# The end of a two-layer perceiver kernel split by batch, with one eviction rule and one order of queries changed

## The chip, the cores and the metric

One core of a Trainium2 chip runs the whole program. The metric is the device time of one execution in microseconds, as the median of several. TensorE (PE), VectorE (DVE), ScalarE (ACT), GpSimd (POOL) and SyncE (SP, which only starts transfers here) run side by side and wait for each other by semaphores; there is no other order between them.

## The reference, cut to what matters

Two layers over x of 2 batches x 128 rows x 256 columns. All edits lie in layer 1 (and the last part of layer 0's feed-forward stands just ahead of it).

```python
x = x + _L1_xattn_ref(_layernorm(x), ctx_2048, ...)   # 16 heads of 16, all 4096 context keys, int8-like rounding
x = x + _L1_attn_ref(_layernorm(x), ...)              # two positions per row, causal: row 0 sees itself only
x = x + _L1_ffn_ref(_layernorm(x), ...)               # router, shared MLP of 1024, routed MLP of 128
return x
# _L1_attn_ref: position 0 of the causal pair has output = its own value; position 1 needs q, both k, both v
# _L1_ffn_ref:
logits = x @ router_weight.T
topk_vals, topk_idx = top_k(logits, 2)
comb_w = sum(softmax(topk_vals) * (topk_idx < 8))
shared = (g * sigmoid(g) * u) @ sh_down.T             # g, u = x @ sh_gate.T, x @ sh_up.T
routed = (same with r_gate, r_up, r_down) * comb_w
```

In the self-attention of layer 1 the two batches of the kernel are the two positions. So batch 0 needs only its own value, while batch 1 needs its queries and the keys and values of both.

## The kernel before, in words

The kernel is written out by hand: each engine has one list of instructions, in the order in which its function bodies (L600 to L2071) issue them. An engine never overtakes itself; a wait at the head of a list stops all that stands behind it.

**Ahead of the attention (L1841 to L1883).** `columns(k, b)` turns the normalised rows `xn` of batch b by two transposes and ScalarE copies them (L728) to `xnT`. `queries(b)` (L1846) multiplies them with the query weights; `integer_queries(b)` on VectorE (L1357) rounds them; `query_columns(b)` turns them. `value_rows(n)` (L1854) turns eight blocks of the values, and ScalarE copies them out (L973). The TensorE order is columns(3,0), value_rows(0), queries(0), value_rows(1), columns(3,1), value_rows(2), query_columns(0), queries(1), then scores(0,0). ScalarE copies columns(3,0), then runs one dummy exponential at L968, which loads the table for what follows, then goes on to L973.

**The cross-attention (L1885 to L1978).** A unit is one head of one batch, `UNITS` = 32 of them, batch the faster index. Per unit: `scores(u, c)` for four chunks of 1024 keys (two products of 512 columns each, L1897), read on VectorE by `maxima(u, c)` (L1387), which scales, keeps the maximum and stores; GpSimd combines the four maxima (L693 to L697); ScalarE makes the exponentials as bytes (L1002); a quarter (c = 0, 1, 2) is turned by TensorE in `turned_over` (L1921) and the last quarter by a DMA transpose started by SP (L583). The turned quarters stand in PSUM in three banks used in turn and are moved out by `columns16`, either on VectorE (L1398) or on ScalarE (L1017); `on_vector(u, c)` (L77) says which. `weighted(u, c)` (L1929 to L1948) multiplies them with the values: 8 products when VectorE moved the quarter (it subtracts 1024 on the way) and 16 when ScalarE did (the subtraction is then done by 8 products with -1024). VectorE works on maxima two units ahead of the quarter that TensorE turns. SP also brings the scales of head h+2 (L568, two halves of 1 MB) as the buffer of head h becomes free.

**Behind the attention (L1981 to L2071 on TensorE, L1415 to L1486 on VectorE, L1027 to L1060 on ScalarE).** Everything starts once unit 31 is done. The reciprocals of all 32 sums, both batches' rows scaled (L1420), turned (L1985), copied (L1029), multiplied by the output weights (L1991), added to `xres` (L1429), normalised (add, stats at L1079, aggregate, GpSimd's power at L609, scale at L1071), turned (L1499), copied (L728), then the five products of the self-attention (L1997). Batch 1's attention is VectorE work (L1435 to L1453) with one exponential (L1047). Then each batch goes through turn (L2017), copy (L1043), output product (L2024), add (L1458), normalise, turn, copy, logits (L2044). Only then come the experts: nine steps k (routed block first, then eight shared blocks), each with gate and up products over 256 columns, which are both batches (L2058, 8 records), a tanh on ScalarE (L1060), two VectorE instructions (L1475, L1477). They use four PSUM banks in turn. The routed down product is L2063, the shared one L2069 for batch 0 and then batch 1; VectorE adds them to `xres` and SP writes it out.

`awake(n)` (L1490) issues n products of 512 columns whose result nobody reads. There are 29 of them behind the attention, in six places.

## Time and profile before

| | us |
|---|---|
| runs shown | 439.37 to 440.07, median 439.52 |
| the profiled execution, whole | 442.38 |
| its span | 440.6 |
| PE busy | 408.4 (93%) |
| DVE busy | 357.3 (81%) |
| ACT busy | 303.0 (69%) |
| POOL busy | 105.3 (24%) |

The whole execution is 1.78 us longer than the span, which runs from the first to the last instruction. Busy time of PE counts the full depth of each product, and products overlap, so its 93% does not say that it is at its limit. Times in rows are microseconds from the start of the span; "x16" is how many instructions a row merges; what stands in square brackets is the idle time of the engine before the row and what ended it.

### The profile page before, as it was taken

The numbers are of one execution on the slowest core, as the hardware profiler recorded it, in microseconds if no ns is written. First come the engines' busy times: TensorE is split into PE (matmuls) and PEld (weight loads), VectorE is DVE, ScalarE is ACT, GpSimd is POOL, SyncE is SP. The second block draws the span as 40 slices with busy tenths as digits, with TensorE's granted clock in tenths as the row PEclk, the third lists the DMA queues.
The fourth block names the chain that finished last, engine by engine and source line by source line (L and its number), as shares of the span: only waits on it lengthen the run. The fifth ranks groups of instructions, "written<-read, shape, count | busy, mean of one in ns | idle before, by whom it ended". The sixth has DMA issues, their size and how long they took to land.

```text
span 440.6 us, 9345 instructions
## 1 busy us (share of the span) xinstructions
PE 408.4 (93%) x3822; PEld 297.9 (68%) x3822; DVE 357.3 (81%) x582; ACT 303.0 (69%) x382; POOL 105.3 (24%) x177
## 2 busy tenths in 40 slices
PE   8989899999999999999789999999999999888897
PEld 4878778855555554576347777777777777755686
DVE  2846662879999999987899999999999999654343
ACT  3245834788888776553789999999999999811110
POOL 3100402044444444001245333321111111100000
PEclk9999999999999999999989999999999999889899
DMA  7898912411001100369488789999999894300000
GB/s 281 295 425 301 196 70 73 192 32 31 25 27 27 31 3 0 140 227 438 210 243 249 251 274 263 243 255 251 250 220 311 203 273 101 51 1 0 1 1 24
DMA packets 48245, 71.46 MB, mean 162 GB/s; under 512 B 38954, under 2 KB 41674, under 8 KB 42698
## 3 DMA queue, kind: packets, MB, share of 16 engines
q1 hardware_dynamic: 47626, 67.32, 51.4%
q0 software_dynamic: 576, 3.54, 2.1%
q8 instruction: 30, 0.49, 0.5%
q14 instruction: 13, 0.11, 0.1%
HBM read 61.58 MB, written 1.15 MB: 142 GB/s over the span
## 4 chain that ended last, share of the span: by engine, by line
PE 43%; DVE 41%; issue 7%; ACT 4%; DMA 3%; SPq 1%; DVEq 0%; ACTq 0%
DVE arena L1387 20%; DVE w L1387 9%; PE ps L1671 6%; PE ps L1781 5%; PE ps L1680 5%; PE ps L2058 4%; DVE arena L1398 3%; PE ps L1564 2%; PE ps L1628 2%; DMA arena<-in_segg 2%; PE ps L1720 2%; PE ps L2069 2%; PE ps L1588 1%; PE ps L1493 1%; PE ps L1837 1%
## 5 line engine op out<-in xcount | busy, mean ns | idle before, releaser
L1387 DVE CUSTOM_DVE_ANT_0 arena<-ps,arena 128x1024 f32<-128x1024 f32 x88 | 107.5, 1277 | 0.1
L1897 PE MATMUL ps<-arena 128*128 128x512 bf16 x256 | 77.6, 384 | 11.0 <-DVE arena L1387 7.4
L1002 ACT ACTIVATE arena<-arena 128x4096 uint8<-128x4096 f32 x21 | 78.0, 3716 | 7.8 <-POOL arena L697 7.8
L1921 PEld LDWEIGHTS ps<-cst,arena 128*128 128x128 f32 x384 | 48.2, 144 | 23.2 <-ACT arena L1002 7.2
L1921 PE MATMUL ps<-cst,arena 128*128 128x128 f32 x384 | 59.8, 280 | 2.7 <-ACT arena L1017 2.1
L1941 PE MATMUL ps<-vrow,arena 128*128 128x16 f16 x806 | 52.6, 170 | 0.5 <-ACT w L1017 0.5
L1941 PEld LDWEIGHTS ps<-vrow,arena 128*128 128x128 f16 x806 | 49.2, 96 | 3.9 <-ACT w L1017 0.6
L1387 DVE CUSTOM_DVE_ANT_0 w<-ps,arena 128x1024 f32<-128x1024 f32 x40 | 49.6, 1276 | 0.0
L1944 PE MATMUL ps<-vrow,arena 128*128 128x16 f16 x768 | 45.8, 170 | 0.0
L672 POOL TENSOR_TENSOR arena<-arena 128x1024 f32<-128x1024 f32 x14 | 33.0, 2358 | 39.2 <-DVE arena L1276 39.2
L1944 PEld LDWEIGHTS ps<-vrow,arena 128*128 128x128 f16 x768 | 40.9, 98 | 1.4 <-DVE arena L1398 0.3
L1002 ACT ACTIVATE arena<-w,arena 128x4096 uint8<-128x4096 f32 x10 | 37.1, 3714 | 3.6 <-POOL arena L697 3.6
L693 POOL TENSOR_SCALAR arena<-arena 128x1 f32<-128x1 f32 x32 | 11.7, 366 | 113.8 <-DVE arena L1387 113.7
L1276 DVE TENSOR_TENSOR_SCAN arena<-arena 128x1024 f32<-128x1024 f32 x16 | 37.2, 2363 | 0.2
L1017 ACT ACTIVATE arena<-ps 128x512 f32<-128x512 f32 x70 | 36.9, 589 | 0.0
L1671 PE MATMUL ps<-w,arena 128*128 128x256 f32 x128 | 29.4, 380 | 0.2 <-ACT ps L858 0.2
L1680 PE MATMUL ps<-arena,w 128*128 128x512 f32 x64 | 29.4, 600 | 0.0
L1897 PEld LDWEIGHTS ps<-arena 128*128 128x128 bf16 x256 | 15.6, 97 | 19.7 <-DVE arena L1387 9.7
L926 ACT ACTIVATE arena<-arena 128x254 f32<-128x254 f32 x64 | 27.0, 494 | 0.8 <-DVE arena L1257 0.7
L1781 PE MATMUL ps<-arena,cst 128*128 128x512 f32 x60 | 27.2, 594 | 0.3 <-DVE arena L1287 0.3
L1671 PEld LDWEIGHTS ps<-w,arena 128*128 128x128 f32 x128 | 23.9, 190 | 4.2 <-issue 0.5
L609 POOL TENSOR_TENSOR ln_rs<-ln_ve,neghalf 128x1 f32<-128x1 f32 x12 | 6.6, 554 | 74.7 <-DVE ln_ve L1083 74.7
(278 smaller groups left out, 743.8 us busy)
## 6 DMA issues: line engine op xcount, KB each, us to landing
arena<-ks_scr SPq DMA_DIRECT2D x32, 1024.0 KB, 5.6
arena<-in_w SPq DMA_DIRECT2D x1, 4488.0 KB, 22.1
arena<-in_columns SPq DMA_DIRECT2D x4, 1024.0 KB, 7.8
arena<-in_w0b SPq DMA_DIRECT2D x1, 2560.0 KB, 16.7
w<-in_w SPq DMA_DIRECT2D x1, 2286.0 KB, 10.8
arena<-in_w SPq DMA_DIRECT2D x1, 2048.0 KB, 7.7
arena<-in_fill SPq DMA_DIRECT2D x1, 2048.0 KB, 9.1
arena<-bc_scr SPq DMA_DIRECT2D x14, 128.0 KB, 3.0
```

The costliest lines, as they stand in the source:

```text
L672: pool.tensor_tensor(dbx[:, s], u[:, :, :], bcb[:, n % 4, :].unsqueeze(1).broadcast_to([P, ET, T]), ALU.mult)\
L1002: act.activation(out8[:, :, 0], s_sb[u % 3], ACT.Exp, bias=nb[:, u % 3:u % 3 + 1], accum_out=zall[:, u:u + 1]).then_inc(p_ready, 1)
L1017: act.activation(columns.bitcast(F32), bank(4 + n % 3, 0, 512), ACT.Copy).then_inc(ptr_sb[1], 1)
L1276: dve.tensor_tensor_scan(hst[:, s, :], dA[:, s].rearrange("p t n -> p (t n)"), dbx[:, s].rearrange("p t n -> p (t n)"), 0.0, ALU.mult, ALU ...
L1387: dve.tensor_tensor_reduce(s_sb[slot][:, keys], ps[:, 2 * (c % 2):2 * (c % 2) + 2, :].rearrange("p a n -> p (a n)"), ksb[h % 2][:, keys], ...
L1671: mm = pe.matmul(bank(k_at + a, t * D, D), vT[:, c, i * CK + k:i * CK + k + P], w_kv[:, c, 0:D], start=False, stop=(c == CH - 1), skip_gro ...
L1680: mm = pe.matmul(bank(m, 0, CK), w_kv[:, c, D + m * P:D + (m + 1) * P], vT[:, c, i * CK:(i + 1) * CK], start=(c == 0), stop=(c == CH - 1))
L1781: mm = pe.matmul(bank(6 + n, 0, 512), ident, rows[:, n * 512:(n + 1) * 512], start=False, stop=True, skip_group_check=True)
L1897: mm = pe.matmul(bank(2 * (c % 2) + m, 0, 512), qz[h // 8][:, h % 8, b * L:(b + 1) * L], kT[:, h // 8, k:k + 512], start=True, stop=True)
L1921: mm = pe.transpose(bank(4 + n % 3, k * P, P), words[:, w:w + P], ident)
L1941: pe.matmul(bank(7, u * HW, HW), neg1024[:, :], vrow[:, h // 2, v:v + HW], start=False, stop=False)
L1944: mm = pe.matmul(bank(7, u * HW, HW), turned, vrow[:, h // 2, v:v + HW], start=(t == 0), stop=(t == KT - 1))
```

## The change

Three things are changed.

1. `on_vector(u, 0)` is true for even u instead of for u mod 3 < 2 (and stays true for units 30 and 31). For units 0 to 29 that is 15 quarters on VectorE instead of 20; the five others go to ScalarE, with 8 more small products each on TensorE.
2. Ahead of the attention, TensorE issues queries(1), query_columns(0), value_rows(2) instead of value_rows(2), query_columns(0), queries(1). The dummy exponential stands ahead of columns(3,0) on ScalarE.
3. All that follows the attention is written per batch. Batch 0's rows are scaled when unit 30 is done; its turning and its output product stand between the pieces of unit 31, whose result goes to a bank of its own. The self-attention of batch 0 is ahead of batch 1's queries. The experts run as ten steps, five per batch (the routed block alone, then four pairs of blocks, 128 columns each), over two PSUM banks; steps 0 to 4 stand among the instructions of batch 1's self-attention, output and norm. The six `awake` calls (29 products) are replaced by one of three.

```diff
+STEPS = ((FT,), *((m, m + 1) for m in range(0, FT, 2)))
+NS = len(STEPS)
...
-    return (u % 3 < 2 or u >= LAST - 1) if c == 0 else ((u == LAST - 1 and c < TURNED) or (u == LAST and c < 3))
+    return (u % 2 == 0 or u >= LAST - 1) if c == 0 else ((u == LAST - 1 and c < TURNED) or (u == LAST and c < 3))
...
+            act.activation(spare[:, :], spare[:, :], ACT.Exp)
             columns(3, 0)
-            act.activation(spare[:, :], spare[:, :], ACT.Exp)
...
-                for c in range(4 if unit == LAST else TURNED):
+                for c in range(TURNED):
                     if not on_vector(unit, c):
...
+            context_columns(0)
+            columns16(LAST, 3)
+            context_columns(1)
             columns(4, 0)
-            columns(4, 1)
             act.wait_ge(pe_step, VALUE0_MADE)
             act.activation(orow[:, 0, :], bank(5, 0, D), ACT.Copy).then_inc(oa_first, 1)
...
+            def gate_of(k):
+
+                width = len(STEPS[k % NS]) * L
                 act.wait_ge(moe_gu, k + 1)
                 if k >= 2:
                     act.wait_ge(moe_h, k - 1)
-                act.activation(tg[:, k % 2, :], bank(k % 4, 0, T), ACT.Tanh, scale=0.5).then_inc(moe_t, 1)
+                act.activation(tg[:, k % 2, 0:width], bank(k % 2, 0, width), ACT.Tanh, scale=0.5).then_inc(moe_t, 1)
+
+            def shares(b):
+
+                act.wait_ge(te_arg, b + 1)
+                act.activation(te[:, b, :], te[:, b, :], ACT.Exp).then_inc(te_ready, 1)
+
+            self_columns(0)
+            columns(4, 1)
+            act.wait_ge(pe_step, Q_MADE)
+            act.activation(q1[:, :], bank(2, 0, D), ACT.Copy, scale=HW ** -0.5).then_inc(q1_sb, 1)
+            columns(5, 0)
+            act.wait_ge(e2_arg, 1)
+            act.activation(e2[:, :, :], s2[:, :, :], ACT.Exp).then_inc(e2_ready, 1)
+            gate_of(0)
+            shares(0)
+            gate_of(1)
+            self_columns(1)
+            gate_of(2)
+            gate_of(3)
+            columns(5, 1)
+            gate_of(4)
+            shares(1)
+            for k in range(NS, 2 * NS):
+                gate_of(k)
...
+            for unit in range(LAST):
                 for c in range(4):
...
-            columns16(LAST, 1)
-            columns16(LAST, 2)
+            heads = onrm.rearrange("q b (h d) -> q b h d", d=HW)
+            made = bank(7, 0, 512).rearrange("q (h b d) -> q b h d", h=H, b=B)
+            sums, shares = (t.rearrange("q (h b) -> q b h", b=B) for t in (zall, rz))
+
+            def context(b):
+
+                dve.wait_ge(ptr_used, 4 * (LAST + b))
+                link(dve.reciprocal(shares[:, b], sums[:, b]))
+                if b:
+                    dve.tensor_tensor(heads[:, b, H - 1:H], bank(2, 0, HW).unsqueeze(1),
+                                      shares[:, b, H - 1:H].unsqueeze(2).broadcast_to([P, 1, HW]), ALU.mult)
+                n = H - b
+                dve.tensor_tensor(heads[:, b, 0:n], made[:, b, 0:n], shares[:, b, 0:n].unsqueeze(2).broadcast_to([P, n, HW]), ALU.mult)\
+                   .then_inc(on_rows, 1)
+
+            def measured(k, b):
+
+                link(dve.bn_stats(ln_st[:, b, :], xres[:, b, :]))
+                link(dve.bn_aggr(ln_mv[:, b, :], ln_st[:, b, :]))
+                dve.tensor_scalar(ln_ve[:, b:b + 1], ln_mv[:, b, 1:2], EPS, None, ALU.add).then_inc(ln_var, 1)
+
+            def normal(k, b):
+
+                dve.wait_ge(ln_rstd, B * k + b + 1)
+                dve.tensor_scalar(xn[:, b, :], xres[:, b, :], ln_mv[:, b, 0:1], ln_rs[:, b:b + 1], ALU.subtract, ALU.mult)\
+                   .then_inc(ln_rows, 1)
+
+            def crossed(b):
+
+                dve.wait_ge(added_out, (X_OUT0, X_OUT1)[b])
+                link(dve.tensor_tensor(xres[:, b, :], bank((1, 6)[b], 0, D), xres[:, b, :], ALU.add))
+                measured(4, b)
+
+            def attended_self(b):
+
+                dve.wait_ge(added_out, (SA_OUT0, SA_OUT1)[b])
+                link(dve.tensor_tensor(xres[:, b, :], bank((4, 3)[b], 0, D), xres[:, b, :], ALU.add))
+                measured(5, b)
+
+            def routes(b):
+
+                dve.wait_ge(pe_step, (LOGITS0, LOGITS1)[b])
+                link(dve.max(top[:, b, :], bank(7, b * E, E)))
+                dve.tensor_tensor(te[:, b, :], top[:, b, 0:2], top[:, b, 0:1].broadcast_to([P, 2]), ALU.subtract).then_inc(te_arg, 1)
+
+            def weights_of(b):
+
+                dve.wait_ge(te_ready, b + 1)
+                link(dve.tensor_tensor(tz[:, b:b + 1], te[:, b, 0:1], te[:, b, 1:2], ALU.add))
+                link(dve.reciprocal(tz[:, b:b + 1], tz[:, b:b + 1]))
+                link(dve.tensor_tensor(te[:, b, :], te[:, b, :], tz[:, b:b + 1].broadcast_to([P, 2]), ALU.mult))
+                link(dve.tensor_tensor(comb[:, b:b + 1], te[:, b, 0:1], te[:, b, 1:2], ALU.add))
+
+            def hidden(k):
+
+                b, blocks = k // NS, STEPS[k % NS]
+                n = len(blocks)
+                dve.wait_ge(moe_t, k + 1)
+                link(dve.scalar_tensor_tensor(out=ga[:, k % 2, 0:n * L], in0=tg[:, k % 2, 0:n * L], scalar=1.0,
+                                              in1=bank(k % 2, 0, n * L), op0=ALU.add, op1=ALU.mult))
+                dve.scalar_tensor_tensor(out=hT[:, blocks[0]:blocks[0] + n, b * L:(b + 1) * L],
+                                         in0=ga[:, k % 2, 0:n * L].rearrange("p (m l) -> p m l", m=n), scalar=0.5,
+                                         in1=bank(k % 2, T, n * L).rearrange("p (m l) -> p m l", m=n),
+                                         op0=ALU.mult, op1=ALU.mult).then_inc(moe_h, 1)
+
+            def routed(b):
+
+                dve.wait_ge(routed_out, b + 1)
+                link(dve.scalar_tensor_tensor(out=xres[:, b, :], in0=bank((5, 4)[b], 0, D), scalar=comb[:, b:b + 1], in1=xres[:, b, :],
+                                              op0=ALU.mult, op1=ALU.add))
+
+            def finished(b):
+
+                dve.wait_ge(moe_out, b + 1)
+                dve.tensor_tensor(xres[:, b, :], bank((2, 3)[b], 0, D), xres[:, b, :], ALU.add).then_inc(y_ready, 1)
+
+            context(0)
+            for c in range(3):
+                columns16(LAST, c)
             dve.wait_ge(p_ready, UNITS + 2)
...
-            normalise(4, crossed)
+            crossed(0)
+            context(1)
+            normal(4, 0)
+            crossed(1)
+            normal(4, 1)
+            attended_self(0)
+            normal(5, 0)
...
+            routes(0)
...
-            normalise(5, attended_self)
...
+            hidden(0)
+            hidden(1)
+            weights_of(0)
+            hidden(2)
+            attended_self(1)
+            normal(5, 1)
+            hidden(3)
+            hidden(4)
+            routes(1)
+            hidden(NS)
+            weights_of(1)
+            for k in range(NS + 1, 2 * NS):
+                hidden(k)
+            routed(0)
+            finished(0)
+            routed(1)
+            finished(1)
...
+            queries(1)
+            query_columns(0)
             value_rows(2)
-            query_columns(0)
-            queries(1)
...
+                if u == LAST and c == 0:
+                    pe.wait_ge(s_read, 4 * UNITS)
...
+                        out = bank(7, u * HW, HW) if u < LAST else bank(2, 0, HW)
...
+            def context_columns(b):
+
+                pe.wait_ge(on_rows, b + 1)
+                for c in range(CH):
+                    mm = pe.transpose(bank((0, 4)[b], c * P, P), onrm[:, b, c * P:(c + 1) * P], ident)
+                mm.then_inc(pe_step, 1)
+
+            def context_out(b):
+
+                pe.wait_ge(on_cols, b + 1)
+                for c in range(CH):
+                    mm = pe.matmul(bank((1, 6)[b], 0, D), onT[:, c, b * L:(b + 1) * L], w_p[:, c, :],
+                                   start=(c == 0), stop=(c == CH - 1))
+                mm.then_inc(added_out, 1)
+
+            def logits(b):
+
+                pe.wait_ge(ln_cols, 5 * B + b + 1)
+                for c in range(CH):
+                    mm = pe.matmul(bank(7, b * E, E), xnT[:, c, b * L:(b + 1) * L], w_rt[:, c, :],
+                                   start=(c == 0), stop=(c == CH - 1))
+                mm.then_inc(pe_step, 1)
+
+            def gates(k):
+
+                b, blocks = k // NS, STEPS[k % NS]
+                if k >= 2:
+                    pe.wait_ge(moe_h, k - 1)
+                for n, w in ((0, w_sg), (1, w_su)):
+                    for i, m in enumerate(blocks):
+                        for c in range(CH):
+                            mm = pe.matmul(bank(k % 2, n * T + i * L, L), w[:, c, m * P:(m + 1) * P], xnT[:, c, b * L:(b + 1) * L],
+                                           start=(c == 0), stop=(c == CH - 1))
+                mm.then_inc(moe_gu, 1)
+
+            def expert(b):
+
+                pe.wait_ge(moe_h, NS * b + 1)
+                pe.matmul(bank((5, 4)[b], 0, D), hT[:, FT, b * L:(b + 1) * L], w_sd[:, FT, :], start=True, stop=True)\
+                  .then_inc(routed_out, 1)
+
+            def down(b):
+
+                for m in range(FT):
+                    if m % 2 == 0:
+                        pe.wait_ge(moe_h, NS * b + 2 + m // 2)
+                    mm = pe.matmul(bank((2, 3)[b], 0, D), hT[:, m, b * L:(b + 1) * L], w_sd[:, m, :],
+                                   start=(m == 0), stop=(m == FT - 1))
+                mm.then_inc(moe_out, 1)
+
             for c in range(4):
                 weighted(LAST - 1, c)
             turned_over(LAST, 0)
-            for c in range(1, 4):
-                turned_over(LAST, c)
-                weighted(LAST, c - 1)
+            context_columns(0)
+            turned_over(LAST, 1)
+            weighted(LAST, 0)
+            turned_over(LAST, 2)
+            weighted(LAST, 1)
+            pe.wait_ge(wp_scaled, CH)
+            context_out(0)
+            turned_over(LAST, 3)
+            weighted(LAST, 2)
             weighted(LAST, 3)
...
-            awake(5)
...
-            awake(6)
...
-            awake(2)
...
-            awake(8)
...
+            awake(3)
+            context_columns(1)
             columns(4, 0)
...
+            context_out(1)
...
+            projected(0, 2, 5).then_inc(pe_step, 1)
+            projected(0, 1, 3)
+            pe.wait_ge(oa_first, 1)
+            self_columns(0)
             columns(4, 1)
-            projected(0, 2, 5).then_inc(pe_step, 1)
+            self_out(0)
...
             projected(1, 0, 2).then_inc(pe_step, 1)
+            columns(5, 0)
+            logits(0)
+            gates(0)
+            gates(1)
             pe.wait_ge(oa_rows, 1)
             self_columns(1)
+            gates(2)
             self_out(1)
-            awake(5)
-            columns(5, 0)
-            awake(3)
+            gates(3)
+            columns(5, 1)
+            gates(4)
+            logits(1)
+            gates(5)
...
+            expert(0)
+            gates(6)
+            gates(7)
+            expert(1)
+            gates(8)
+            gates(9)
+            down(0)
+            down(1)
```

## Rows read from the trace of the kernel before

**Rows 1.** The chain that ended last, shares of the span by engine.
```profile
PE 43%; DVE 41%; issue 7%; ACT 4%; DMA 3%; SPq 1%; DVEq 0%; ACTq 0%
```

**Rows 2.** Stretch, length, busy (x) of PE PEld DVE ACT POOL, PEclk, DMA, GB/s.
```profile
240.00:260.00 20.00, 18.93 (x303) 14.64 (x302) 20.00 (x34) 19.04 (x17) 6.46 (x15) 1.00 0.84 259
```

**Rows 3.** Groups by line and form, 200 to 380 us: count, busy, mean ns, idle.
```profile
L1387 DVE CUSTOM_DVE_ANT_0 arena<-ps,arena 128x1024 f32<-128x1024 f32 x88 | 107.5, 1277 | 0.1
...
L1387 DVE CUSTOM_DVE_ANT_0 w<-ps,arena 128x1024 f32<-128x1024 f32 x40 | 49.6, 1276 | 0.0
...
L1398 DVE TENSOR_SCALAR arena<-ps 128x1024 f16<-128x1024 f16 x20 | 13.7, 683 | 0.0
```

**Rows 4.** Timeline of one unit: start, duration, engine, line, idle before.
```profile
269.54 1.55 ACT L1017 ACTIVATE arena<-ps 128x512 f32<-128x512 f32 x3
...
270.96 3.72 ACT L1002 ACTIVATE arena<-arena 128x4096 uint8<-128x4096 f32 x1
...
271.76 0.69 DVE L1398 TENSOR_SCALAR arena<-ps 128x1024 f16<-128x1024 f16 x1
...
272.36 1.27 DVE L1387 CUSTOM_DVE_ANT_0 w<-ps,arena 128x1024 f32<-128x1024 f32 x1
...
276.06 3.71 ACT L1002 ACTIVATE arena<-w,arena 128x4096 uint8<-128x4096 f32 x1 [0.32 <-POOL arena L697]
```

**Rows 5.** Timeline ahead of the attention, 206 to 213 us.
```profile
206.03 1.28 ACT L968 ACT_TABLE_LOAD   x1
...
207.43 1.00 ACT L973 ACTIVATE vrow<-ps 128x1024 f16<-128x1024 bf16 x1
...
208.34 0.38 ACT L728 ACTIVATE xnT<-ps 128x256 f32<-128x256 f32 x1
...
209.45 1.08 PE L1850 MATMUL ps<-arena,xnT 128*128 128x256 f32 x4
...
210.57 0.42 DVE L1362 TENSOR_REDUCE arena<-ps 128x16 f32<-128x256 f32 x1 [1.30 <-PE ps L1850]
...
212.64 1.28 DVE L1387 CUSTOM_DVE_ANT_0 arena<-ps,arena 128x1024 f32<-128x1024 f32 x1
```

**Rows 6.** Timeline behind the attention, from unit 31 to the experts.
```profile
384.47 1.95 PE L1921 MATMUL ps<-cst,arena 128*128 128x128 f32 x8
...
389.43 0.18 PE L1941 MATMUL ps<-vrow,arena 128*128 128x16 f16 x1 [0.49 <-ACT w L1017]
...
400.73 0.42 DVE L1435 TENSOR_TENSOR arena<-ps,arena 128x256 f32<-128x256 f32 x1 [3.66 <-PE ps L1997]
...
404.57 0.42 DVE L1453 TENSOR_TENSOR arena<-arena 128x256 f32<-128x256 f32 x1
...
407.95 0.42 DVE L1458 TENSOR_TENSOR xres<-ps,xres 128x256 f32<-128x256 f32 x1 [1.76 <-PE ps L2024]
...
412.69 10.56 PE L2058 MATMUL ps<-xnT,arena 128*128 128x256 f32 x40
```

**Rows 7.** Timeline of the end: experts' steps, down products, last add.
```profile
418.11 0.38 ACT L1060 ACTIVATE arena<-ps 128x256 f32<-128x256 f32 x1 [1.34 <-PE ps L2058]
418.52 0.42 DVE L1475 SCALAR_TENSOR_TENSOR arena<-arena,ps 128x256 f32<-128x256 f32 x1 [0.78 <-ACT arena L1060]
...
430.86 7.07 PE L2069 MATMUL ps<-arena 128*128 128x256 f32 x32
...
437.97 0.42 DVE L1486 TENSOR_TENSOR xres<-ps,xres 128x256 f32<-128x256 f32 x1 [2.96 <-PE ps L2069]
```

**Rows 8.** Timeline: a run of products of 128 columns, 32.7 to 37.2 us.
```profile
32.75 4.37 PE L1564 MATMUL ps<-vrow,arena 128*128 128x128 f32 x36
```

**Rows 9.** Stretches around the two falls of the clock, columns as in Rows 2.
```profile
382.00:388.50 6.50, 6.50 (x112) 5.95 (x110) 3.47 (x6) 3.02 (x6) 0.00 (x0) 0.50 0.00 0
...
389.00:412.50 23.50, 18.95 (x104) 12.11 (x104) 10.75 (x34) 4.27 (x12) 2.21 (x4) 1.00 0.00 1
412.50:416.20 3.70, 3.70 (x12) 3.04 (x13) 1.06 (x7) 0.21 (x1) 0.00 (x0) 0.54 0.00 0
```

140 lines of the change are left out of this document (32 added, 108 removed).

## Prediction

> **What bounds the kernel now.** I read the chain of waits first: PE 43% and DVE 41% of it, so two engines take turns and the question is where [rows 1]. The stretches answer it. From 212.64 us, where the first maximum starts [rows 5], VectorE has no idle time: 20.00 of 20 us while PE, ACT and the DMAs have some left [rows 2]. 128 maxima and 20 turned quarters fill its list, with 0.1 us idle in all [rows 3]. One quarter costs it 0.60 us, from the start of the quarter to the start of the next maximum; the mean of 683 ns in the groups is longer because ends overlap with the next start [rows 3, 4]. Behind the attention the chain is serial: hand-overs between PE, VectorE, ScalarE and GpSimd for batch 1, up to 412.69, then TensorE alone with the experts until 437.97 [rows 6, 7]. So what is worth anything there is work of batch 0 that can be done while batch 1's hand-overs run.
>
> I work out all times on the clock of the profiled execution (span 440.6, whole 442.38) and take the difference off the median of 439.52, which is 2.86 lower than that execution.
>
> **Quarters moved to ScalarE.** 20 - 15 = 5 quarters x 0.60 = 3.0 us off VectorE's list, if nothing else is late. Is ScalarE? Three quarters take it 270.96 - 269.54 = 1.42 us, 0.47 each, and one exponential 3.72 [rows 4]. A unit with two quarters is 4.66 us, with three 5.14; the mean of alternating units is 4.90. VectorE needs 4 x 1.205 = 4.82 or, with a quarter, 5.42, mean 5.12. So ScalarE is 0.3 us late behind each three-quarter unit (5.14 against the 4.82 that VectorE takes then) and gets 0.76 back in the next. Today it does the same every third unit and VectorE does not notice: the exponential at 270.96 comes straight behind three quarters, without a wait, and the next one already waits 0.32 for GpSimd again [rows 4]. TensorE gets 8 products of 16 columns more per moved quarter. Their price is between 0 and that of passes of 128 columns, 0.117 each [rows 8], so at most 0.9 us; I take a quarter of that, since the work of 16 columns is an eighth and something is fixed. It falls into units in which VectorE takes 5.42 us, and in every third unit TensorE does just this today. The DMAs carry the same bytes in a unit 0.1 us shorter: their share of 0.84 [rows 2] goes to 0.86. The bounds: 0 (something just hidden becomes the bound) to 3.0; I take 3.0, since each of the two kinds of unit already stands in today's trace without idle time of VectorE.
>
> **Queries moved up.** VectorE's second rounding starts at 210.57 and waited 1.30 us for TensorE; the product starts at 209.45, so 1.12 lie between [rows 5]. Its operand was copied at 208.34 + 0.38 = 208.72; behind that stood value_rows(2) and query_columns(0), whose inputs came later. Now queries(1) starts right behind the copy: 208.78. And the copy comes earlier: ScalarE ran the table load of 1.28 us at 206.03, in front of the first value rows at 207.43 [rows 5]; with the dummy exponential moved it falls in the idle time before 205.6. The copy at 208.34 then waits only for its transposes, and I put it at 207.96. So queries(1) at 208.4 and the rounding at 209.55: 1.0 us earlier. What is late next is the first rounding, which ends at 209.3, so no more can be had. VectorE goes straight on to the maxima: all of 1.0 us is passed on. Without the earlier copy it is 0.6; bounds 0.6 to 1.1.
>
> Together VectorE ends the maxima 4.0 us earlier. Below I leave these 4.0 out and subtract them at the end.
>
> **Unit 31 with batch 0 in between.** The stretch 382.0 to 388.5 runs at a granted clock of 0.50, that is 1.2 GHz [rows 9]; there eight transposes need 1.95 us, 0.21 each [rows 6]. Batch 0's scaling starts when unit 30's products end (384.6) and takes VectorE 0.7; TensorE waits for it 0.1 and does two transposes, 0.4. The output product is 4 passes, 0.43 each at the low level and 0.215 at the high one (the 32 passes in 7.07 us [rows 7]); with the clock's rise at 388.6 in the middle of them 1.2. The last quarter's product, at 389.43 now [rows 6], starts at 390.5: **1.1 us lost**.
>
> **From there to batch 1's first attention product.** Today 400.73 - 389.43 = 11.3 us [rows 6]. In it both batches' norms alternate on VectorE, and of the five self-attention products three stand between batch 1's turned rows and the keys that VectorE awaits. In the new order batch 0's add and statistics are done in the wait for unit 31, the two products of batch 0 that matter are issued earlier, and in their place batch 0's output product (0.86) stands. I follow it hand-over by hand-over with today's durations (add 0.42, statistics to root 1.4, copy 0.38, four passes 0.86): rows scaled 392.0, output product of batch 1 ready 394.2, its norm 396.2, queries 398.9, keys 399.7, VectorE free at **400.4**. So 0.3 us ahead of today, with the loss already paid. Bounds 399.5 to 401.5.
>
> **Batch 1's attention to its norm.** VectorE's list is the same 3.84 us plus 0.4 for batch 0's router, part of it in the wait for the exponential: rows made at 404.75 + 0.4 (today 404.57 + 0.42 [rows 6], call both 405.0). TensorE in this time does batch 0's logits, step 0 (0.94) and step 1 (1.87). Then gates(2) stands in front of self_out(1): 1.9 us of TensorE that batch 1's chain has to wait out, while the hand-over that it fills takes 0.7. And hidden(2) stands in front of the add on VectorE. The add comes at 408.9 instead of 407.95: **1.0 us lost**. Then the norm, with hidden(3) behind it; TensorE ends gates(3) at 410.1, idles 1.2 us, turns batch 1's rows at 411.3 and begins gates(4) at 411.6.
>
> **What the experts' overlap is worth.** At 411.6 steps 0 to 3 are behind, 0.94 + 3 x 1.87 = 6.55 us of TensorE. What is left: steps 4, 6, 7, 8, 9 at 1.87 = 9.35, step 5 0.94, logits 0.5, two routed products 0.86, down 32 x 0.2155 = 6.9: 18.55 us, and 0.25 to the last add: 430.4 instead of 437.97 [rows 7]. **7.6 us gained**, losses above included. Where a step's 1.87 comes from: a pass over 128 columns takes (4.37 - 0.27) / 35 = 0.117 us [rows 8], so 16 of them 1.87; today's pass over 256 takes 0.2155 [rows 7], half of it 0.108. Splitting by batch loads each weight twice and costs 144 x 0.117 - 72 x 0.2155 = 1.3 us, which is in the sum. Two banks instead of four: step k waits for VectorE's step k-2. A step's end to its hidden rows takes 0.2 + 0.41 + 0.90 = 1.5 us (tanh at 418.11, VectorE at 418.52, its two instructions 0.9 [rows 7]), less than the 1.87 of the step between: hidden, by 0.3 us only. Part of the 7.6 is that today's first step stands in a fall of the clock: 412.5 to 416.2 at 0.54 [rows 9] costs 1.7 us, and I count no such fall in the new kernel, where 10 us of products run almost without a gap before that point.
>
> The sum: 3.0 + 1.0 + 7.6 = **11.6 us**. Span 429.0, whole 430.8, median 439.52 - 11.6 = **427.9**.
>
> **Rivals.**
> *A: a fall of the clock comes back among the experts.* 29 filling products become 3. For: with 29 of them the clock still fell at 412.5, behind a stretch with gaps; the new kernel has gaps at 391 to 393, 401 and 410. Against: from 389.0 to 412.5, with PE busy for 18.95 of 23.5, the clock stayed at 1.00 [rows 9], and dense products brought it back within 3.7 us. Price of one fall 1.7: 429.6. A rule bears on this. In 382.0 to 388.5 PE counts as busy for the whole 6.50 us and still has half the clock; the work is mostly transposes and 16-column products [rows 9]. The Trainium skill ("TensorE: Matmul & The Clock Gate", section Part 4: PE-mode transpose) says that a transpose does not count as busy for the gate in the way a product does. By that rule the transposes put between unit 31's pieces help nothing, and the filling products taken out were what held the clock; that is this rival, and its time by rows is the 429.6 above.
> *B: the two banks serialise the steps.* The margin of 0.3 us is gone where weights_of or a norm stands in VectorE's list. If six of ten steps wait 0.4 us more, 2.5 us: 430.4. For: VectorE and ScalarE serve both batches in one fixed order. Against: after 417 VectorE has only the steps.
> *C: the loop gives nothing.* ScalarE's lateness reaches VectorE through TensorE: 3.0 us less, 430.9. For: ScalarE rises to 4.90 of 5.12. Against: rows 4, as above.
> *D: unit 31 runs at the full clock* because the phase has moved by 4 us: 2 us better, 425.9.
> *E, the other side: the clock stays at 1.2 GHz from 391 us on*, since no filling products lift it. TensorE's 27 us of products behind 401 then take 54, less some 2.5 of waits: 24.5 us more than forecast, 452, slower than before. It decides once more than 11.6 us of work are lost so, that is 23 us at the low level. Against: dense products ended the low stretch at 416.2 [rows 9].
>
> **How the numbers follow.** Forecast 0.53; A 0.14; B 0.14; C 0.08; D 0.08; E 0.03. Time 427.9. The range goes from 425.6 (D, a little more) to 432.0 (A and B together, or C with part of A). About 0.2% (0.9 us) is what can be told from no change. Faster: all but E and 0.01 for a mishap of that size: 0.96; same 0.01; slower 0.03.
>
> **What would show it.** First maximum at 211.6; last one ends at 375.1; no idle time of VectorE between; the last quarter's product 1.1 us later relative to that; batch 1's first attention product 21.3 us behind the last maximum (today 21.6); a pass of the experts at 0.117; TensorE without gaps over 0.5 us from gates(4) on; down products of 6.9 us at the end. Wrong would be a wait of VectorE for TensorE's scores in odd units, granted clock 0.50 behind 391, or waits of gates(k) for VectorE longer than 0.5.

## The result, and the profile after

In the first comparison, four executions of each, the kernel after takes 429.30 us (428.01 to 430.04) and the one before 439.44 (439.28 to 440.07): ratio 0.974, 95% interval 0.969 to 0.978, 10.1 us faster by the medians. (The ratios in this text are estimates over all executions of a comparison, so they need not be the quotient of the two medians, which is 0.977 here.) Forecast were 11.6 us and 427.9; 429.3 lies in the range. A second set gave 429.67 (six executions, 428.78 to 430.84) and a ratio of 0.971 (0.967 to 0.976). The profiled execution of after took 428.01, span 426.2; what lies around the span is 1.8 us, as before.

The page of the kernel after: the span, busy time by engine, the granted clock in 40 slices, and the shares of the chain that ended last.

```profile
span 426.2 us, 9529 instructions
PE 400.1 (94%) x3908; PEld 295.1 (69%) x3908; DVE 354.9 (83%) x586; ACT 305.4 (72%) x389; POOL 105.4 (25%) x177
PEclk9999999999999999999989999999999999999999
DVE 43%; PE 40%; issue 8%; ACT 4%; DMA 3%; SPq 1%; POOL 0%; POOLq 0%; DVEq 0%; ACTq 0%
```

The chain has the same two engines in front as in [rows 1]. Stretches of the kernel after, columns as in [rows 2]: one of the loop, the low stretch in it, the loop as a whole from 225, the work behind it.

```profile
240.00:260.00 20.00, 19.23 (x318) 14.67 (x316) 20.00 (x35) 19.36 (x19) 7.36 (x16) 1.00 0.90 265
...
221.50:224.50 3.00, 3.00 (x13) 2.20 (x12) 3.00 (x6) 2.46 (x1) 1.36 (x3) 0.51 1.11 254
225.00:375.00 150.00, 143.14 (x2320) 109.63 (x2318) 149.46 (x250) 144.97 (x133) 40.59 (x104) 1.00 0.94 239
375.00:425.50 50.50, 44.68 (x419) 39.42 (x419) 26.38 (x80) 13.65 (x33) 2.73 (x6) 1.00 0.05 12
```

VectorE is full as before, PE has gone from 18.93 to 19.23 of 20 and ScalarE from 19.04 to 19.36. From 225 us on the clock is 1.00 to the last product: this execution has no low stretch there. The one at 221.5, at 1.2 GHz, costs nothing that shows, since VectorE works through it.

The groups by line of the loop (line 1407 are the maxima, 1387 before; 1418 the quarters that VectorE turns, 1398 before; 18 fall into the 200 to 380 us shown, 20 of them before):

```profile
L1407 DVE CUSTOM_DVE_ANT_0 arena<-ps,arena 128x1024 f32<-128x1024 f32 x88 | 107.7, 1284 | 0.0
...
L1407 DVE CUSTOM_DVE_ANT_0 w<-ps,arena 128x1024 f32<-128x1024 f32 x40 | 49.4, 1284 | 0.0
L1418 DVE TENSOR_SCALAR arena<-ps 128x1024 f16<-128x1024 f16 x18 | 12.4, 691 | 2.3 <-PE ps L2021 2.3
```

The maxima have no idle time; the 2.3 us belong to unit 30's three quarters, which VectorE turns behind the last maximum. The timeline ahead of the attention and in one unit:

```profile
207.85 1.13 PE L1924 MATMUL ps<-arena,xnT 128*128 128x256 f32 x4 [0.47 <-ACT xnT L731]
...
209.02 0.42 DVE L1382 TENSOR_REDUCE arena<-ps 128x16 f32<-128x256 f32 x1 [0.24 <-PE ps L1924]
...
211.09 1.28 DVE L1407 CUSTOM_DVE_ANT_0 arena<-ps,arena 128x1024 f32<-128x1024 f32 x1
...
268.49 3.71 ACT L1005 ACTIVATE arena<-arena 128x4096 uint8<-128x4096 f32 x1 [0.31 <-POOL arena L700]
...
272.20 1.55 ACT L1020 ACTIVATE arena<-ps 128x512 f32<-128x512 f32 x3
...
273.63 3.72 ACT L1005 ACTIVATE arena<-w,arena 128x4096 uint8<-128x4096 f32 x1
```

TensorE's second queries start 1.60 us earlier than in [rows 5], VectorE's second rounding waits 0.24 for them instead of 1.30, and the first maximum starts at 211.09 instead of 212.64. Of that 1.55, 0.49 is the stage in front, which happened to be earlier. In the unit shown, three quarters put ScalarE straight in front of its next exponential, as in [rows 4], and no maximum waits.

The timeline behind the loop, with what answers to [rows 6, 7]. Line 2018 is the start of unit 31's last quarter's product (1941 before), 1524 batch 1's first attention product on VectorE, 1543 its rows made, 1468 its self-attention add, 2101 the gates, 2116 the down products, 1506 the last adds.

```profile
384.83 0.18 PE L2018 MATMUL ps<-vrow,arena 128*128 128x16 f16 x1 [0.51 <-ACT w L1020]
...
394.39 0.42 DVE L1524 TENSOR_TENSOR arena<-ps,arena 128x256 f32<-128x256 f32 x1
...
398.22 0.42 DVE L1543 TENSOR_TENSOR arena<-arena 128x256 f32<-128x256 f32 x1
...
401.11 1.03 PE L2081 MATMUL ps<-arena 128*128 128x256 f32 x4
...
401.98 1.95 PE L2101 MATMUL ps<-xnT,arena 128*128 128x128 f32 x16
...
402.59 0.42 DVE L1468 TENSOR_TENSOR xres<-ps,xres 128x256 f32<-128x256 f32 x1
...
405.00 0.44 PE L1573 MATMUL ps<-cst,xn 128*128 128x128 f32 x2 [1.08 <-DVE xn L1456]
405.28 1.95 PE L2101 MATMUL ps<-xnT,arena 128*128 128x128 f32 x16
...
412.85 3.73 PE L2101 MATMUL ps<-xnT,arena 128*128 128x128 f32 x32
...
416.42 7.07 PE L2116 MATMUL ps<-arena 128*128 128x256 f32 x32
...
423.60 0.42 DVE L1506 TENSOR_TENSOR xres<-ps,xres 128x256 f32<-128x256 f32 x1 [2.64 <-PE ps L2116]
```

Batch 0's experts run amid batch 1's chain. TensorE's only wait of weight there is the 1.08 us at 405.00; from 405.28 it has none. 32 passes over 128 columns take 3.73 us, 0.117 each.

### The same two traces cut into segments

The starts and ends above, read in the same way from every profile of this study, give this table (us; "low" is where the granted clock is at 1.2 GHz behind the loop; A: first maximum's start; B: from there to the last maximum's end; C: from there to batch 1's first attention product; D: from there to its self-attention add; E: from there to the last add, start to start; tail: from the last maximum's end to the span's end).

```
kernel profiled           A       B      C      D      E     tail    low behind the loop
before                  212.64  166.5  21.60  7.22  30.02  61.47   382-388.6, 412.2-416
before again            212.08  166.4  21.27  7.22  28.33  59.40   379.3-382.6
before, VectorE rule    212.57  163.3  20.10  7.21  28.33  58.25   none
before, queries         211.41  166.4  23.77  7.22  30.01  63.59   379.3-393, 413-416.5
before, queries again   211.64  166.4  19.96  7.21  30.02  59.76   410-413.6
before, no fillers      212.52  166.4  26.91  7.06  30.64  67.20   380-404.7, 411-421.7
after, tail alone       212.23  166.4  21.10  8.19  21.01  52.86   381-387.6
after                   211.09  163.4  19.93  8.20  21.01  51.74   none
after again             211.22  163.3  20.91  8.20  21.00  52.70   375.2-378.5
after, no queries       212.63  163.7  19.89  8.19  21.01  51.72   none
after, add ahead        211.31  164.3  19.92  6.46  21.98  50.95   none
after, experts behind   211.77  163.3  21.25  7.51  29.54  60.95   377-383.6, 401-411
every third unit        211.21  162.6  19.96  6.46  21.97  50.94   none
every fourth unit       211.20  163.4  19.68  6.47  21.96  50.66   none
```

Segments B to E repeat to 0.15 us where the order of work and the clock are the same, with three exceptions: in B a pause of VectorE of 0.95 us at 262.95 in "add ahead" and one of 0.21 at 325.02, where it waits for ScalarE's exponential, in "no queries", and in C 0.25 us less in "every fourth unit". Between executions of one kernel it is the clock that differs, and most of all in the last unit of the attention (segment C).

### The profile page after: what moved, and what is told of

It reads as the page before. It is cut to its first block, busy times and chain, and to the rows that moved or that the text cites. A ratio compares the mean times of both kernels' runs of the same rounds, so it can differ in the third digit from the quotient of the medians.

```text
span 426.2 us, 9529 instructions
## 1 busy us (share of the span) xinstructions
PE 400.1 (94%) x3908; PEld 295.1 (69%) x3908; DVE 354.9 (83%) x586; ACT 305.4 (72%) x389; POOL 105.4 (25%) x177
## 4 chain that ended last, share of the span: by engine, by line
DVE 43%; PE 40%; issue 8%; ACT 4%; DMA 3%; SPq 1%; POOL 0%; POOLq 0%; DVEq 0%; ACTq 0%
DVE arena L1407 22%; DVE w L1407 10%; PE ps L1745 6%; PE ps L1855 5%; PE ps L1754 5%; PE ps L2101 2%; DVE arena L1418 2%; PE ps L1638 2%; PE ps L1702 2%; PE ps L1794 2%; PE ps L2116 2%; DMA arena<-in_segg 2%; PE ps L1662 1%; DMA w<-arena 1%; PE ps L1911 1%
## 5 line engine op out<-in xcount | busy, mean ns | idle before, releaser
L1995 PEld LDWEIGHTS ps<-cst,arena 128*128 128x128 f32 x384 | 47.0, 142 | 25.4 <-ACT arena L1005 10.3
L2018 PE MATMUL ps<-vrow,arena 128*128 128x16 f16 x841 | 54.9, 169 | 0.6 <-ACT w L1020 0.5
L2018 PEld LDWEIGHTS ps<-vrow,arena 128*128 128x128 f16 x841 | 51.0, 96 | 4.1 <-ACT w L1020 0.6
L2021 PE MATMUL ps<-vrow,arena 128*128 128x16 f16 x768 | 46.5, 169 | 0.1
L2021 PEld LDWEIGHTS ps<-vrow,arena 128*128 128x128 f16 x768 | 41.3, 97 | 1.3 <-DVE arena L1418 0.3
L1020 ACT ACTIVATE arena<-ps 128x512 f32<-128x512 f32 x75 | 39.5, 593 | 0.0
L1005 ACT ACTIVATE arena<-w,arena 128x4096 uint8<-128x4096 f32 x10 | 37.2, 3717 | 2.0 <-POOL arena L700 2.0
L1296 DVE TENSOR_TENSOR_SCAN arena<-arena 128x1024 f32<-128x1024 f32 x16 | 37.2, 2362 | 0.2
## 6 DMA issues: line engine op xcount, KB each, us to landing
arena<-in_fill SPq DMA_DIRECT2D x1, 2048.0 KB, 10.1
```

The lines of the kernel that those rows point to most:

```text
L1005: act.activation(out8[:, :, 0], s_sb[u % 3], ACT.Exp, bias=nb[:, u % 3:u % 3 + 1], accum_out=zall[:, u:u + 1]).then_inc(p_ready, 1)
L1020: act.activation(columns.bitcast(F32), bank(4 + n % 3, 0, 512), ACT.Copy).then_inc(ptr_sb[1], 1)
L1296: dve.tensor_tensor_scan(hst[:, s, :], dA[:, s].rearrange("p t n -> p (t n)"), dbx[:, s].rearrange("p t n -> p (t n)"), 0.0, ALU.mult, ALU ...
L1995: mm = pe.transpose(bank(4 + n % 3, k * P, P), words[:, w:w + P], ident)
L2018: pe.matmul(out, neg1024[:, :], vrow[:, h // 2, v:v + HW], start=False, stop=False)
L2021: mm = pe.matmul(out, turned, vrow[:, h // 2, v:v + HW], start=(t == 0), stop=(t == KT - 1))
```

## The experiments

**The kernel before again** (no edit).

> The kernel before once more, with nothing changed: it shows how far two samples of one kernel lie apart, and what TensorE's clock did in its profiled execution. Theory (the missing 1.5 us is in the base of the sum): the profiled execution on which the prediction was worked out was 2.9 us above its own median because of the two low stretches of the clock, 382.0 to 388.5 and 412.5 to 416.2; another execution of the same program at its usual 439.4 lacks at least one of them, so its tail from the last maximum to the end takes 58.5 to 59.8 instead of 61.5. Rival (the low stretches belong to the kernel, and the 2.9 are something that the profiler adds elsewhere): both low stretches stand there again, tail 61.3 to 61.6.

Measured: 440.99 median of 12, where the 29 executions of before that stand against it in that comparison have 439.25; ratio 1.001 (0.997 to 1.006). So medians of 12 of one kernel can lie 1.7 us apart. Its stretches, columns as in [rows 2]:

```profile
379.30:382.60 3.30, 3.28 (x44) 3.18 (x45) 1.12 (x2) 3.30 (x5) 0.29 (x2) 0.53 0.44 84
383.00:436.00 53.00, 47.43 (x330) 36.84 (x325) 23.93 (x69) 9.56 (x26) 2.22 (x4) 1.00 0.01 3
```

One low stretch, half as long as in [rows 9], and none ahead of the experts: tail 59.40 instead of 61.47, in the band of the theory. Segment E is 28.33 instead of 30.02, so the low stretch at 412 costs 1.69. The single executions of the kernel before, 69 in the three later comparisons, show the same spread: those with a mean granted clock of 0.995 or more take 438.4 to 440.8, those at 0.98 some 444. Eleven of the 69 had a mean granted clock of 1.00, so no low stretch anywhere, and they take 438.6 to 439.5, in the middle 439.2: just under the 439.44 that the kernel before has in the first comparison. The execution on which the forecast was worked out, 442.38 at 0.984, is one of the longer ones.

**VectorE's rule alone.**

```diff
-    return (u % 3 < 2 or u >= LAST - 1) if c == 0 else ...
+    return (u % 2 == 0 or u >= LAST - 1) if c == 0 else ...
```

> The kernel before with one edit: VectorE turns a quarter in every second unit instead of in two of three. Theory: 5 quarters less at 0.60 us each, 3.0 us faster, 436.4, the loop from first to last maximum 163.4 instead of 166.5 us. Rival (ScalarE is late behind its three-quarter units and this reaches VectorE): less than 2 us faster, 437.5 or more, with idle time of VectorE between maxima.

Measured: 437.89 (12 executions, 436.09 to 441.39), ratio 0.995 (0.991 to 1.000). By the trace, loop 163.3, no idle time between maxima: the theory. By the medians only 1.4 us, which is the rival's number without its mechanism; the interval, 0.2 to 3.9 us, holds both. Its profile is also the only one of before's tail with the clock at 1.00 all through, so it gives the base for equal clocks, 58.25:

```profile
375.00:417.00 42.00, 35.88 (x324) 27.21 (x321) 20.32 (x59) 13.18 (x29) 3.11 (x7) 1.00 0.04 7
```

**The queries alone**, twice: queries(1) ahead of query_columns(0) and value_rows(2), the dummy exponential ahead of columns(3, 0).

```diff
             columns(3, 1)
+            queries(1)
+            query_columns(0)
             value_rows(2)
-            query_columns(0)
-            queries(1)
```

> The kernel before with the second batch's queries and the dummy exponential moved up, nothing else. Theory: the first maximum starts 1.06 us earlier relative to the stage ahead of it and all of it is passed on: 438.4. Rival (it is given back, because the loop is then ahead of its transfers or of TensorE): 439.4, with idle time of VectorE in the first units.

Measured: 439.48 (12 executions), ratio 0.998 (0.994 to 1.002). The first maximum starts at 211.41, and no maximum waits, but the profiled execution, 443.23, one of the two longest, has the longest low stretch of any kernel with fillers:

```profile
379.30:393.00 13.70, 13.07 (x180) 10.70 (x177) 5.49 (x11) 5.76 (x10) 0.00 (x0) 0.50 0.10 20
```

> The kernel before with the queries and the dummy exponential moved up, a second time, since its first profile fell on an execution with 14 us of low clock in the last unit. Theory (the head start of 1.0 us reaches the last maximum and what is behind it is as in before at equal clock): first maximum at 211.4, last one ends at 377.8, and a tail of 58.2 to 59.4 unless a low stretch stands in it; executions without low clock 437.9. Rival (the head start shifts the last unit so that it falls into a low stretch more often): the profile again has a low stretch of over 5 us behind 378 and the median is at or above before's.

Measured: 439.73 (12 executions, the lowest 437.88), ratio 1.000 (0.996 to 1.004). First maximum 211.64, last one's end 378.04, tail 59.76 with only the low stretch ahead of the experts, whose price is again E = 30.02 against 28.33. So the head start reaches the end of the loop in both profiles and is not taken back by a wait; whether the shifted last unit meets low stretches more often, two profiles don't say. In whole times this part alone shows no gain.

**The split alone**: the kernel after with the old rule and the old order of the queries.

> The kernel after with the quarters' rule and the order of the queries as before: only the work behind the last attention is split by batch. Theory (the prediction's 7.6 holds 1.7 for a fall of the clock that the usual execution of before does not have): 5.9 to 6.3 us faster than before, 433.3. Rival (the overlap gives all of 7.6, and what is missing is in the loop): 431.8. The three parts together, this one and the two of the other runs, should make 10.1 us if they do not touch each other.

Measured: 433.56 (6 executions, 431.85 to 433.87), ratio 0.981 (0.976 to 0.986), 5.7 us below before's 439.25 of the same comparison; theory 433.3, rival 431.8. Its trace has before's kind of low stretch in the last unit (6.6 us at 0.50, tail 52.86), none behind it. The three parts alone make 1.4 - 0.2 + 5.7 = 6.9 by the medians of this comparison, and together 10.1; each has an interval of 1.6 to 2.2 us to either side, so I read no interaction from that. By the segments they add up: 3.1, 1.0 and 6.5 us make 10.6.

**The kernel after again** (no edit).

> The kernel after once more, unchanged, for more executions of it beside more of before. Theory (the profiled execution of after had TensorE's full clock from 225 us to its end, and its other executions, 1.3 us longer, do not): median 428.7 to 429.5, 9.9 to 10.4 below before's; where its profile has a low stretch of the clock in the last unit, its tail from the last maximum to the end is longer than 51.74 us by 1 to 2. Rival: the differences between executions lie ahead of the attention or in the loop; then the tail is 51.7 with or without a low stretch.

```profile
375.20:378.50 3.30, 3.18 (x44) 3.09 (x45) 1.12 (x2) 3.30 (x5) 0.38 (x2) 0.56 0.43 83
379.00:425.00 46.00, 42.00 (x372) 36.83 (x368) 24.95 (x78) 9.73 (x28) 2.21 (x4) 1.00 0.01 4
```

Measured: 429.67, 0.2 above the theory's range. The profile has a low stretch in the last unit, and its tail is 52.70 against 51.74, all of it in segment C: the theory's mechanism, at the lower end of its 1 to 2 us. In that comparison, on another chip than the first, the kernel before took 443.67 in the median, so 14.0 more and not the 9.9 to 10.4 forecast; six of its eleven executions took 443.6 or more, at a granted clock of 0.981 to 0.985, and after no more than 430.84, at 0.992 or more. In the profiles the old tail has low stretches in two places, the last unit and just ahead of the experts, and the new one only in the first.

**After without the move of the queries.**

> The kernel after with the order of the queries and the dummy exponential as before. Theory: the first maximum starts 1.1 us later than in after and the end with it: 430.3. Rival (the head start is taken back behind the attention, as the time of the same edit done alone hints, 0.2 us where 1.0 was expected): within 0.3 us of after, with the first maximum later all the same and a tail that is shorter by as much.

Measured: 430.10 (6 executions), 0.4 above after of the same comparison. First maximum at 212.63, 1.4 later; tail 51.72 against after's 51.74, with the clock at 1.00 in both tails. Nothing is taken back behind the attention; the theory's mechanism stands, its 1.1 us is not resolved in the medians.

**After with batch 1's add ahead.**

```diff
             self_columns(1)
-            gates(2)
             self_out(1)
+            gates(2)
             gates(3)
```

and on VectorE attended_self(1) ahead of hidden(2).

> The kernel after with one swap: TensorE does batch 1's self-attention output product ahead of gates(2), not behind it, and VectorE its add ahead of hidden(2). Theory (the prediction's own loss of 1.0 us): the add comes 1.0 us earlier, 7.2 instead of 8.2 us behind batch 1's first attention product; the 1.08 us in which TensorE waits for batch 1's norm ahead of columns(5, 1) stay about as they are, because the same work is done by then in another order, but TensorE now waits 0.6 for the turned rows' copy ahead of the output product; net 0 to 0.5 us faster. Rival (this order costs nothing as TensorE's work is the bound here): 0.5 slower, since TensorE's new wait adds up.

```profile
400.79 1.13 PE L2081 MATMUL ps<-arena 128*128 128x256 f32 x4 [0.47 <-ACT arena L1047]
401.76 3.73 PE L2101 MATMUL ps<-xnT,arena 128*128 128x128 f32 x32
402.03 0.43 DVE L1468 TENSOR_TENSOR xres<-ps,xres 128x256 f32<-128x256 f32 x1
...
405.42 0.44 PE L1573 MATMUL ps<-cst,xn 128*128 128x128 f32 x2
405.69 1.95 PE L2101 MATMUL ps<-xnT,arena 128*128 128x128 f32 x16
```

Measured: 428.38 (6 executions), 1.3 below after of the same comparison, with ratios to before of 0.967 (0.963 to 0.972) and 0.971 (0.967 to 0.976) whose intervals overlap; so it is the trace that shows the gain. The add comes 6.46 behind the first attention product, 1.7 earlier and not 1.0; TensorE waits 0.47 for the copy and no longer 1.08 for the norm. D and E together are 28.44 against 29.21: 0.77 faster, more than the theory's upper end, and the same in the two later kernels that hold this order.

**After with the first batch's experts behind the chain**: gates(0) to gates(3) moved behind columns(5, 1), and the steps' order on ScalarE and VectorE with them.

> The kernel after with the first batch's four expert steps not amid batch 1's chain but behind it: steps 0 to 3 come after batch 1's columns, in the order of each engine; split by batch as in after. It tells what the overlap alone is worth. Theory: TensorE has the 6.55 us of those steps to do behind the chain; the chain of batch 1 without them ends 1.0 us earlier than with them, and 0.3 go to the fillers that are not there: 5.3 to 5.8 us slower than after, which is 434.8. Rival (most of the gain behind the attention comes from the shorter chain of hand-overs by splitting norms and output products, not from the experts amid it): under 4 us slower.

```profile
384.00:400.80 16.80, 12.28 (x94) 9.23 (x92) 10.57 (x37) 3.66 (x10) 1.67 (x3) 1.00 0.01 1
401.00:411.00 10.00, 6.99 (x28) 5.94 (x28) 2.35 (x9) 1.04 (x3) 0.55 (x1) 0.50 0.01 2
```

Measured: 437.27 (6 executions), ratio to before 0.988 (0.983 to 0.993), 7.6 above after of the same comparison. More than 5.8: without batch 0's products TensorE is busy for 12.28 of 16.80 us, then the clock falls for 10 us. D + E is 37.05, 7.8 more than after's. Without the overlap D + E is even longer than before's 35.54 at full clock, and what this kernel still gains is the loop and the queries. So all of the split's gain is the overlap, and some 2 us of it is, as an estimate (7.8 less the 5.3 to 5.8 expected without a fall), the clock that the overlapped products hold up; no run has this order with the clock at 1.00.

**Before without its 29 filling products.**

> The kernel before without the 29 filling products behind the attention (those at 5, 6, 2, 8, 5 and 3; results of theirs are read by nobody). It tells what the clock does without them. Theory, after the variant with the experts behind the chain showed a low stretch of 10 us from 400.9 on, in which VectorE worked at batch 1's attention and TensorE waited: the fillers held the clock there, and without them the stretch at 1.2 GHz returns between the keys' product and the first expert step; it costs its share of the work done in it, some 3 to 5 us, so 443 where before is at 439, tail from the last maximum 62 to 66. Rival (the prediction's 'no clock fall from 391 on'; the fillers do nothing for the clock in this stretch, and only a wait they themselves cause goes away): 438.5 to 439.5, tail 58 to 59.5.

```profile
380.20:404.70 24.50, 20.99 (x203) 17.02 (x201) 8.59 (x21) 7.12 (x13) 1.12 (x2) 0.51 0.06 12
404.80:411.20 6.40, 3.73 (x18) 2.55 (x17) 4.64 (x15) 1.27 (x4) 0.00 (x0) 1.00 0.00 0
411.30:421.70 10.40, 8.03 (x24) 5.76 (x24) 2.98 (x13) 0.97 (x3) 1.10 (x2) 0.51 0.00 0
```

Measured: 446.16 (6 executions), ratio 1.012 (1.007 to 1.017), 6.7 slower, above the 3 to 5 expected; tail 67.20 in a profile that is the longest of the six. The low stretch that starts in the last unit, as in other profiles, goes on for 24.5 us, and a second one stands ahead of and in the experts. The fillers hold the clock, more than I expected. The kernel after has 3 and no low stretch behind 388 in any of the profiles that have the overlap: their place is taken by products that have to be done anyway.

**Versions beyond both**: the add ahead, and VectorE's quarter in every third or fourth unit.

```diff
-    return (u % 2 == 0 or u >= LAST - 1) if c == 0 else ...
+    return (u % 3 == 0 or u >= LAST - 1) if c == 0 else ...
```

> A version meant to be faster than both kernels: after, with batch 1's self-attention output product ahead of gates(2) (tail 50.95 us in the earlier run against 51.74 of after), and VectorE turning its quarter in every third unit, not in every second. By the sum: VectorE 4.82 + 0.60 / 3 = 5.02 a unit, ScalarE 2/3 x 5.14 + 1/3 x 4.66 = 4.98, 5 quarters less. Theory (VectorE still is the bound, by 0.04): loop 160.4 instead of 163.3 us, 425.4 to 425.9 us in all. Rival (within 0.04 of each other two engines hold each other up at every hand-over): loop 161.5 to 163.3, VectorE idle between maxima, 427 to 428.5.

> As the run with every third unit, but VectorE turns a quarter in every fourth unit only: VectorE 4.97 a unit, ScalarE 3/4 x 5.14 + 1/4 x 4.66 = 5.02, so ScalarE is the bound by the sum. Theory (the longest engine sets the loop): 30 units of 5.02 against 5.12 today, loop 160.4, no faster than with every third unit, and now VectorE with waits of 0.05 a unit for ScalarE or for TensorE behind it. Rival (ScalarE has margins that its busy time hides, and VectorE stays the bound): loop 159.2. Second rival (hand-overs add up): 162 or more.

Stretch 340 to 360 us of the one with every third, and with every fourth:

```profile
340.00:360.00 20.00, 18.50 (x312) 14.50 (x315) 19.80 (x34) 19.76 (x19) 3.52 (x12) 1.00 0.99 260
```

```profile
340.00:360.00 20.00, 18.65 (x321) 14.61 (x325) 19.79 (x32) 19.76 (x20) 3.30 (x11) 1.00 0.93 261
```

Measured: 427.91 and 427.61 (6 executions each), ratios 0.971 (0.966 to 0.976) and 0.971 (0.966 to 0.975) to before's 439.42. Both are below after's two medians, by 1.4 to 2.1 us, but the ratios to before don't part them from after (0.974 and 0.971). Where executions at a clock of 0.995 or more are compared, they take 426.6 to 427.3 and 427.1 to 428.8, after 428.0 to 429.5. 0.8 of the difference is the add ahead, seen in three traces. The loop is 162.6 and 163.4, not 160.4, so in both it is the rival with the hand-overs that came true: VectorE no longer runs at 20.00 of 20 and ScalarE has 0.24 left. The sum by the longest engine holds for every second unit and not further: another 3 us in the sum brought 0.8 with every third unit and nothing with every fourth. That is what rival C of the prediction feared, one step further on; through which wait it comes I have not followed.

## Why the prediction was right, and where its sizes were off

**Quarters moved to ScalarE, 3.0.** Right: the loop is 3.1 us shorter in four of the six profiles with the rule (163.3 to 163.4 against 166.4 to 166.5; the other two have 163.7 and 164.3, the latter with the pause at 262.95), and in after's profile VectorE's maxima have no idle time. PE's price does not show: busy for 18.93 of 20 us [rows 2] at 166.5 / 32 = 5.20 us a unit is 4.92 a unit, and 19.23 of 20 at 163.4 / 32 = 5.11 is 4.91; I had taken 0.23 for each moved quarter, which is 0.04 a unit in the mean. Products of 16 columns start 0.025 us apart in after's trace (16 of them from 376.62 to 376.99), so eight more are 0.20. Rival C did not happen, but for one wait of 0.21 us of VectorE for ScalarE in one of the six profiles.

**Queries moved up, 1.0.** Right in the trace: first maximum at 211.09 to 211.77 in the eight profiles with the edit, mean 211.4, and 212.08 to 212.64 in six without, mean 212.4. In whole times the edit alone was within its interval of nothing.

**Unit 31, 1.1 lost; up to the first attention product, 0.3 gained in all.** The forecast put this product 21.3 behind the last maximum with the clock at 0.50 in the last unit. With such a stretch it is 21.10 and 20.91, where before has 21.60 and 21.27 with stretches of the same lengths: 0.5 and 0.4 gained. Without one it is 19.89 to 19.93 (rival D's event, which the profiled execution has, though its time is not), and before has 20.0 to 20.1: 0.0 to 0.2 gained. The forecast's net is right, and both of its parts were too small. The last quarter's product starts 10.30 behind the last maximum in before and 11.55 in the kernel with the split alone, with the same 6.6 us at low clock: 1.25 lost, not 1.1; without a low stretch 8.8 (VectorE's rule alone) and 10.4, so 1.6. From there to the attention product it is 9.56 instead of 11.30 in both cases where I had 9.9.

**Batch 1's add, 1.0 lost.** Segment D is 8.20 against 7.22, and the reason was the one given: with the product and the add moved ahead it is 6.46. But the forecast's 1.0 was net of the 0.3 gained before; for D alone it had 408.9 - 400.4 = 8.5. The 0.3 too much lies ahead of batch 1's rows: they are done 4.25 us behind the first attention product, as in before, where I had 4.6 with 0.4 for the router in it. From there to the add it is 3.95, forecast 3.9.

**The experts' overlap.** Forecast from the add to the last add: 430.4 - 408.9 = 21.5 us; it took 21.01. A pass is 0.117; TensorE has no wait from gates(4) on (rival B did not happen, the margin of 0.3 was enough); down is 7.07 where the list said 6.9. I had 18.8 from gates(4) to the last add and it is 18.3.

**The step that was mis-sized is the base: 7.6 us for the work behind the attention.** It is the difference to one profiled execution, and 1.7 of it is that execution's low stretch at 412.5. The price was right (30.02 against 28.33 is 1.69). What failed is taking this off the median of 439.52: the prediction says that the execution is 2.86 longer than that median, and never asks whether the fall counted as a gain is part of those 2.86. The runs say that it is. In the repeated profile of the same kernel, 439.73, the fall isn't there, and the eleven executions of before without any low stretch take 439.2 in the middle, so there is no room for 1.7 in a median of 439.4 to 439.5. (The fall is no rarity: both profiles with the queries moved up have it. What the first four executions of before had in this place, no trace shows.)

Like for like, with the clock at 1.00 in both tails, the tail goes from 58.25 to 51.74: 6.5 us. With a low stretch of 3.3 us in the last unit of both it goes from 59.40 to 52.70, 6.7. With the loop's 3.1 and the queries' 1.0 the 6.5 make 10.6, against 10.1 measured on medians of which both hold some low stretches. Without the 1.7 the forecast would have been 9.9, and 429.6, next to the 429.3 measured. Part of that nearness is luck: the terms behind the attention were 0.6 to 1.0 too pessimistic (0.3 in D and 0.5 in E, as above, and -0.1 to 0.2 in C), which hid as much of the 1.7. Rival A's time is 429.6 as well, but its mechanism, a fall among the experts, is in no profile of after or of its variants with the overlap.

**Rival E and the rule on transposes.** The danger was real, if much smaller than E's 24.5 us, and was averted. The two kernels in which TensorE's gaps are left unfilled show it: with the experts behind, 10 us at 1.2 GHz from 401 on, and without the fillers 35 us in two stretches, for 6.7 us of time. By the Trainium skill, "TensorE: Matmul & The Clock Gate", section Part 4: PE-mode transpose, transposes don't count as products do for the gate; the low stretches in the last unit, where PE counts as busy throughout [rows 9] with 24 transposes and 88 products of 16 columns, agree with it, but no run here took the transposes out, and in 7 of the 14 profiles, after's among them, the last unit has no low stretch.

**Open.** Why one execution has a low stretch in the last unit and the next has none; and why the parts alone gain less in whole times than in the traces. Six or twelve executions a kernel, with a spread of up to 6 us, don't settle the second.

## What to carry to other kernels

Before a difference is taken off a median, look where the profiled execution is above that median; a stretch at half clock that the change "removes" may not be in the others at all. Work of one batch put into another's chain of hand-overs pays twice, by its own length and by the clock that it holds up, and what it may not do is stand in front of the product that the chain waits for. In this loop ScalarE at 97% of the time, beside VectorE at 100%, cost nothing, while moving still more work until the two were within 1% by the sum brought 0.8 us of 3.0, or nothing.

## What the runs showed of the hardware

- A low stretch of TensorE's clock that begins in the last unit lasted 3.3, 6.6, 13.7 or 24.5 us in profiles of kernels with the same work there, and in half of the profiles there was none. Its price depends on what waits: 1.0 to 1.3 us for 3.3 in the last unit, 1.2 to 1.6 for 6.6, 3.7 to 3.8 for 13.7, 1.69 for the 3.7 us ahead of and in the experts, and nothing that shows for the 3 us at 221.5, where VectorE was the bound.
- 29 products whose results nobody reads are worth 6.7 us of 439: without them 35 us behind the loop ran at 1.2 GHz.
- The same program took 439.25 in the median in one comparison and 443.7 in another, on another chip; in the first, 6 of 29 executions had a mean granted clock of 0.985 or less, in the second 7 of 11.
